# Causal attention of a fused four-stage kernel: its order of work across batches, its first scores and its start are rearranged

## What is computed

```python
q = frac_rope(einsum('btm,mhd->bhtd', x, wq)) * 128 ** -0.5    # H = 2 heads, D = 128
k = frac_rope(einsum('btm,mhd->bhtd', x, wk)) * 128 ** -0.5
v = einsum('btm,mhd->bhtd', x, wv)
s = einsum('bhid,bhjd->bhij', q, k) - 1e30 * (i < j)
p = softmax(s)
o = einsum('bhij,bhjd->bhid', p, v)
return einsum('bhid,hdm->bim', o, wo)

x = x + attn_a(layernorm(x))
x = x + ffn(layernorm(x))
x = x + attn_b(layernorm(x))
x = x + ffn(layernorm(x))
```

## Time and profile before

| what | value |
|---|---|
| median of 3 runs | 1931.45 us (1931.37 to 1933.29) |
| profiled execution | 1933.55 us, of which the span of its instructions 1931.8 us |
| granted TensorE clock, mean | 0.998 |
| TensorE busy | 1876.5 us, 97% of the span |
| VectorE busy | 1339.2 us, 69% |
| ScalarE busy | 878.5 us, 45% |
| GpSimd busy | 500.0 us, 26% |
| attention phase | to about 560 us of the span |

### The profile page before, as it was taken

The page is one execution under the profiler, slowest core; times in us unless marked ns, Lnnn a source line. Parts: engine busy times, 40 slices in busy tenths (PEclk is TensorE's granted clock), DMA queues, the critical chain, the costliest instruction groups (busy, mean ns, idle before and its releaser), DMA issues.

```text
span 1931.8 us, 36459 instructions
## 1 busy us (share of the span) xinstructions
PE 1876.5 (97%) x12321; PEld 1620.6 (84%) x12321; DVE 1339.2 (69%) x3141; ACT 878.5 (45%) x1716; POOL 500.0 (26%) x405
## 2 busy tenths in 40 slices
PE   6999999999999999999999999999999999899998
PEld 5778888887888888888888888888888887788887
DVE  5566666566668888766666766676766667788885
ACT  5666556555654444453333333333333332444443
POOL 4222102202222232232322222222222223422210
PEclk9999999999999999999999999999999999999999
DMA  7100000000013221120000000000000001222322
GB/s 240 41 1 0 0 0 0 0 0 0 6 22 84 33 31 29 29 70 10 10 11 10 11 11 11 11 11 11 11 11 11 12 12 15 38 62 62 64 57 54
DMA packets 230598, 53.19 MB, mean 28 GB/s; under 512 B 209664, under 2 KB 228736, under 8 KB 230144
## 3 DMA queue, kind: packets, MB, share of 16 engines
q1 hardware_dynamic: 229264, 49.53, 12.7%
q10 hardware_dynamic: 1264, 2.76, 0.4%
HBM read 18.69 MB, written 8.39 MB: 14 GB/s over the span
## 4 chain that ended last, share of the span: by engine, by line
PE 88%; DVE 4%; issue 2%; SPq 2%; ACT 1%; DMA 1%; POOL 1%; ACTq 0%; DVEq 0%; POOLq 0%
PE PS L324 18%; PE PS L1153 16%; PE PS L1162 9%; PE PS L333 7%; PE PS L815 6%; PE PS L844 6%; PE PS L1617 5%; PE PS L1659 4%; PE PS L1603 3%; PE PS L833 3%; PE PS L1636 3%; PE PS L1623 2%; PE PS L855 2%; SPq L272 2%; PE PS L1591 1%
## 5 line engine op out<-in xcount | busy, mean ns | idle before, releaser
L324 PE MATMUL PS<-ln_xh,lin_w 128*128 128x512 f32 x768 | 248.8, 392 | 0.0
L1090 ACT ACTIVATE ff_silu<-PS 128x512 f32<-128x512 f32 x192 | 114.5, 597 | 235.3 <-PE PS L1153 207.4
L1125 DVE SCALAR_TENSOR_TENSOR ff_h<-PS,ff_silu 128x512 f32<-128x512 f32 x192 | 131.3, 685 | 111.6 <-PE PS L1153 93.0
L1374 POOL TENSOR_TENSOR lin_yg_lo<-stage,lin_yg_hi 128x512 fp32r<-128x512 f32 x64 | 82.3, 1286 | 484.2 <-ACT lin_yg_hi L1392 484.2
L1392 ACT ACTIVATE lin_yg_hi<-stage 128x512 fp32r<-128x512 f32 x64 | 40.5, 633 | 347.4 <-DVE stage L1487 316.1
L1109 DVE TENSOR_TENSOR ff_h_lo<-ff_h,ff_h_hi 128x512 fp32r<-128x512 f32 x192 | 168.4, 877 | 0.4
L324 PEld LDWEIGHTS PS<-ln_xh,lin_w 128*128 128x128 f32 x768 | 144.2, 188 | 28.7
L844 PE MATMUL PS<-probT,v_a 128*128 128x128 f32 x1152 | 153.9, 279 | 3.7 <-DVE oT_lo L705 3.7
L844 PEld LDWEIGHTS PS<-probT,v_a 128*128 128x128 f32 x1152 | 139.0, 192 | 18.7 <-issue 11.1
L1449 DVE TENSOR_TENSOR lin_AD<-PS,lin_decay 128x512 f32<-128x512 f32 x128 | 82.2, 684 | 104.6 <-PE PS L1603 104.6
L324 PE MATMUL PS<-ln_xl,lin_w 128*128 128x512 f32 x384 | 150.1, 391 | 0.0
(11 more groups left out here) (172 smaller groups left out, 5187.8 us busy)
## 6 DMA issues: line engine op xcount, KB each, us to landing
ff_raw<-ln_xn SPq DMA_DIRECT2D x480, 32.0 KB, 2.0
ln_xl<-ln_xn SPq DMA_DIRECT2D x288, 32.0 KB, 1.9
X<-in_x SPq DMA_DIRECT2D x8, 1024.0 KB, 5.5
out_x<-X SPq DMA_DIRECT2D x16, 512.0 KB, 2.9
stage<-in_w_lin SPq DMA_DIRECT2D x1, 2048.0 KB, 8.2
stage<-in_w_gate SPq DMA_DIRECT2D x2, 768.0 KB, 7.4
stage<-in_w_up SPq DMA_DIRECT2D x2, 768.0 KB, 8.9
stage<-in_w_down SPq DMA_DIRECT2D x2, 768.0 KB, 10.3
```

The source lines that it names most:

```text
L324: last = nc.tensor.matmul(out, w, x, start=n == 0, stop=n == len(terms) - 1)
L1090: nc.scalar.activation(silu[:, f % NB_GU, :], PS[:, f % NB_GU, :], ACT.Silu, scale=W_SCALE).then_inc(silu_done.sem, 1)
L1125: nc.vector.scalar_tensor_tensor(h[:, f % 2, :], PS[:, NB_GU + f % NB_GU, :], W_SCALE, silu[:, f % NB_GU, :], ALU.mult, ALU.mult).then_inc ...
```

## The change

- Layernorm signals (statistics, aggregate, power) count once for each group of 4 tiles, and each of these steps is done for one group at a time. In the loop VectorE takes and aggregates group 0 at step 4 and group 1 at step 6.
- Start: x of batch 0 comes in two DMAs with a semaphore each; the identity has a semaphore of its own, and TensorE's first transposes wait for that alone; the first projection waits for two preparations, the other three are waited for before scores 0. VectorE's and ScalarE's preparations are reordered, the first half before `wo` and the mask.
- GpSimd adds the first half in two pieces, tokens 0 to 127 (`first_rotated`) and 128 to 511 (`rotated`).
- TensorE: scores 0 and 1 come before values 0 and 1; scores 0 wait for `first_rotated` and for the swap of projection 4, scores 2 for `rotated`. Values 2 come after scores 2. Transposes 0 and 1 wait for swaps 6 and 7.
- ScalarE: exponential 0 comes before values 0 and swap 7, and the copy of probabilities 0 before values 2.
- Weighted values 15 and output projection 14 of a batch come after the first projection of the next, output projection 15 after the second.
- First batch: squares after steps 8 to 15 and one behind the loop. Last batch: `low_sum` before the statistics, its transpose after projection 2.

```diff
@@ Layernorm
-    def dve_aggregate(self, dve, turn):
-        wait_alone(dve, self.stats_done.sem, self.stats_done.at(turn, 1), self.dve_passed)
-        for t in range(self.tiles):
+    def dve_aggregate(self, dve, turn, group=0):
+        wait_alone(dve, self.stats_done.sem, self.stats_done.at(turn, group + 1), self.dve_passed)
+        for t in range(group * UT, (group + 1) * UT):
...
@@ SP
-            load_x(0)
+            for half in range(NHALF):
+                at = slice(half * UT, (half + 1) * UT)
+                sp.dma_start(X[:, at, :], x_v[:, at, :]).then_inc(x_first[half], 16)
@@ GpSimd
-                        for h in range(HA):
-                            rows = slice(h * ROT, (h + 1) * ROT)
-                            done = nc.gpsimd.tensor_tensor(qk[rows, s, h, at], qk[rows, s, h, at],
-                                                           swapped[rows, 2 * half + s, :], ALU.add)
-                        done.then_inc(rotated.sem, 1)
+                        for some in (slice(0, P), slice(P, UN)) if half == 0 else (slice(0, UN),):
+                            for h in range(HA):
+                                rows = slice(h * ROT, (h + 1) * ROT)
+                                to = qk[rows, s, h, half * UN + some.start:half * UN + some.stop]
+                                done = nc.gpsimd.tensor_tensor(to, to, swapped[rows, 2 * half + s, some], ALU.add)
+                            done.then_inc((first_rotated if some.stop == P else rotated).sem, 1)
@@ ScalarE, start
+            act_decays(nc, act, env, 1)
+            sx[0].act(act, 0)
             act.wait_ge(const_loaded, 16 * N_CONST)
             nc.scalar.activation(wo_hi[:], wo_raw, ACT.Copy).then_inc(prep_hi, 1)
-            act_decays(nc, act, env, 1)
+            sx[1].act(act, 0)
@@ ScalarE, turn
                 for m in range(NPROJ - 1):
                     swap_halves(b, m)
+                exp_step(b, 0)
                 values(b, 0)
                 swap_halves(b, NPROJ - 1)
                 values(b, 1)
-                exp_step(b, 0)
                 for n in range(NS):
                     if n + 1 < NS:
                         exp_step(b, n + 1)
+                    evacuate_probs(b, n)
                     if n == 0:
                         values(b, 2)
-                    evacuate_probs(b, n)
...
-                    if first and n >= NS - NPART:
-                        part = n - (NS - NPART)
...
+                    if first and n > NS - NPART:
+                        square(n - (NS - NPART) - 1)
+                if first:
+                    square(NPART - 1)
                 evacuate_out(b, NS - 1)
@@ VectorE, turn
                 if last:
-                    following.ln.dve_stats(dve, 0)
                     dve.wait_ge(env["ff_squares"], NPART)
                     nc.vector.tensor_reduce(env["low_sum"][:], env["low_squares"][:], AX.X,
                                             ALU.add).then_inc(env["low_summed"], 1)
+                    following.ln.dve_stats(dve, 0)
@@ VectorE, start
+            for half in range(NHALF):
+                dve.wait_ge(x_first[half], 16)
+                ln.dve_stats(dve, 0, half)
             dve_decays(nc, dve, env, 1)
+            dve.wait_ge(prep_hi, 1)
             nc.vector.scalar_tensor_tensor(wqkv_lo[:, :, 0:nq], wqkv_raw[:, :, 0:nq], QK_SCALE,
                                            wqkv_hi[:, :, 0:nq].bitcast(F32), ALU.mult, ALU.subtract).then_inc(prep_done, 1)
+            ln.dve_normalise(dve, 0, 0)
+            dve.wait_ge(prep_hi, 2)
             nc.vector.tensor_tensor(wqkv_lo[:, :, nq:], wqkv_raw[:, :, nq:], wqkv_hi[:, :, nq:].bitcast(F32),
                                     ALU.subtract).then_inc(prep_done, 1)
+            ln.dve_normalise(dve, 0, 1)
+            sx[0].dve(dve, 0)
...
+            sx[1].dve(dve, 0)
             run_batches(dve, turn)
@@ TensorE, scores
-                if i % UT == 0 and h == 0:
+                if n == 0:
+                    pe.wait_ge(first_rotated.sem, first_rotated.at(b, 2))
+                elif n == HA or n == HA * UT:
                     pe.wait_ge(rotated.sem, rotated.at(b, 2 * (i // UT + 1)))
@@ TensorE, turn
-                pe.wait_ge(pt_done.sem, pt_done.at(b, 0))
...
                         if m == 0 and not first:
+                            weighted_values(b, -1)
+                            out_projection(b, -2)
+                        if m == 1 and not first:
                             out_projection(b, -1)
-                        if m == 0 and last:
+                        if m == 2 and last:
...
+                if first:
+                    pe.wait_ge(prep_done, 5)
+                pe.wait_ge(swap_done.sem, swap_done.at(b, NPROJ - 3))
+                scores(b, 0)
+                scores(b, 1)
                 values(b, 0)
                 pe.wait_ge(swap_done.sem, swap_done.at(b, NPROJ - 2))
                 values(b, 1)
-                scores(b, 0)
-                scores(b, 1)
-                values(b, 2)
-                pe.wait_ge(swap_done.sem, swap_done.at(b, NPROJ))
...
                 for n in range(NS):
+                    if n < 2:
+                        pe.wait_ge(swap_done.sem, swap_done.at(b, NPROJ - 1 + n))
                     transpose_probs(b, n)
                     if n + 2 == HA * UT:
                         pe.wait_ge(v_done.sem, v_done.at(b, TB))
                     if n + 2 < NS:
                         scores(b, n + 2)
+                    if n == 0:
+                        values(b, 2)
...
-                else:
-                    last_values()
-
-            pe.wait_ge(const_loaded, 16 * N_CONST)
+
+            pe.wait_ge(ident_loaded, 16)
             for s in sx:
                 s.pe(pe, 0, 0)
-            pe.wait_ge(prep_done, 5)
+            pe.wait_ge(prep_done, 2)
             run_batches(pe, turn)
```

More of the change, by code:

```diff
@@ L484, in attention_phase @@
         const_loaded, w_loaded, x_loaded = sem("a_const_loaded"), sem("a_w_loaded"), sem("x_loaded")
+        ident_loaded, x_first = sem("a_ident_loaded"), [sem(f"x_first{half}") for half in range(NHALF)]
         prep_hi, prep_done = sem("a_prep_hi"), sem("a_prep_done")
@@ L573, in turn @@
                 if not last:
-                    ln.pool_rstd(pool, b + 1)
+                    for half in range(NHALF):
+                        ln.pool_rstd(pool, b + 1, half)
                 else:
@@ L578, in turn @@
                     following.ln.pool_rstd(pool, 2)
-            ln.pool_rstd(pool, 0)
+            for half in range(NHALF):
+                ln.pool_rstd(pool, 0, half)
             run_batches(pool, turn)
@@ L795, in _ @@
             nc.vector.tensor_copy(mask_b[:], mask_f[:]).then_inc(prep_done, 1)
-            for s in sx:
-                s.dve(dve, 0)
+            sx[1].dve(dve, 0)
             run_batches(dve, turn)
```

91 lines of the change are left out of this document (42 added, 49 removed).

## The result

The changed kernel takes **1915.53 us** (median of 4 runs, 1914.17 to 1915.96), the kernel before, run beside it, 1931.41 (4 runs, 1929.85 to 1933.29). The ratio is 0.991, 95% interval 0.9899 to 0.9922. Forecast were 1918.8 and a range of 1912.5 to 1926. The profiled execution took 1915.64 with a span of 1913.9, against 1933.55 and 1931.8.

A forecast was written before the change was run, and what follows sets the result against it. TensorE, busy 97% of the span, was taken as the bound, its attention-phase waits as the room. Gains of 7.35 (batches), 1.9 (squares) and 3.4 (start) make 12.65, from the median 1931.45 to 1918.8 us; range 1912.5 to 1926.

The forecast's parts named there:

- The waits named: TensorE's waits in the attention phase: start, exponentials, attention output's low part, copied probabilities, low_sum; near 27 us in all.
- the signs named: Included no oT_lo wait, some 0.5 us before transpose 0, a new wait before values 3, period 66.2 us.
- Part 1: Deferred last values, run after the next batch's first projection: the 0.53 us wait goes seven times, 0.65 each with refill.
- Part 2: Early first scores with narrow rotation: transpose 1 sooner; with the deferral 1.0 us a batch, bounds 0 and 1.6.
- rival 2: Batch starts: both waits vanish because VectorE and ScalarE are a little quicker; 13.1 us there, 1913.0 us in all; chance 0.12.
- my own case: The whole forecast as summed: 1918.8 us, between 1914.5 and 1923; chance 0.71.
- Rival 1: Batch starts: GpSimd keeps its turn, times_sin(2) waits for all four key additions, nothing gained there; 1926.8 us; chance 0.14.
- Rival 3: GpSimd's narrow addition costs what a wide one does: at 1.3 us each the kernel takes 1956 us; chance 0.03.
- The last batch: Also loses the 0.9 us wait before low_sum, but VectorE's statistics delay the swaps; gain 1.0 us in all.
- Part 3: First batch's squares one step later: TensorE's wait for copied probabilities goes; gain 1.9 us, between 1.0 and 1.9.
- Part 4: Start: first projection at 15.7, 3.0 us earlier, plus 0.4 for the clock; gain 3.4 us, between 2.3 and 5.4.
- Part 5: The rest, such as norm signals by half at steps 4 and 6: cost 0.

The follow-up runs named there:

- n8: n1 plus one added wait: GpSimd adds the wide keys of the first half only after times_sin(2) is done; 1917.24 us.
- n1: Changed kernel with weighted values 15 and output projection 14 back at the end of their batch; 1922.39 us.
- n3: Changed kernel with only the keys of the first half split on GpSimd, the queries added in 512 columns again; 1917.79 us.
- n9: Changed kernel with one added wait alone: GpSimd adds the wide keys of the first half only after times_sin(2); 1915.85 us.
- n2: Changed kernel without the narrow addition: GpSimd adds queries and keys in 512 columns, scores 0 wait for the whole half; 1922.81 us.
- n4: Changed kernel with scores 0 and 1 and exponential 0 back at their old places, split, deferral and start kept; 1917.34 us.
- n7: Changed kernel plus three edits: wide keys wait for times_sin(2), both normalisations before the second low part of the weights, last batch's next-stage statistics at step 2; 1911.60 us.
- n5: Changed kernel with the first batch's squares back after steps 7 to 15; 1920.47 us.
- n10: The changed kernel again, letter for letter; 1915.39 us.
- n11: n7 again, the same program; 1914.82 us.

## Why the prediction was right or wrong

**Direction, range and bound: right.** The waits named were the room, and all of them went but the start's, which shrank. Of the signs named, two did not come: there is no wait before transpose 0, and the period is 65.62 and not 66.2. And one wait sits where the prediction called a wait a sign of being wrong, at scores 0, though in the last batch alone.

**Part 1: right, slightly small.** No wait for `oT_lo`; worth 0.72 a batch by n8, forecast 0.65. What the forecast did not have is that the deferral also shifts VectorE against GpSimd; without it, and without a guard, 0.66 more is lost (n1).

**Part 2 is where the sum fell short.** With Part 1 it gave 1.62 a batch for the 1.0 forecast, and of these 0.62 only 0.07 are Part 1's. The narrow price was right (0.458 for 0.48), and so was the time of the narrow keys. The step that failed is the one that laid `times_sin(1)` behind the whole query set, and with it "`times_sin(2)` enters at 100.95". I gave VectorE the gap at the second set of additions and not at the first, by the same rows. The distance from the first narrow query addition shows it: forecast 95.3 to `times_sin(2)` at 100.95, 5.65; measured 89.42 to 94.03, 4.61. `times_sin(1)` went into the gap between the two wide query additions and ended at 92.03, a full us sooner by the same count than behind the whole set, so the `times_cos` and swaps behind it were 0.6 to 0.85 us earlier, `times_sin(2)` was asked for a full us sooner, and TensorE found transpose 0 ready and values 3 all but ready. n3 is the kernel that I had laid out in this respect: `times_sin(1)` stands behind the whole query set again, and a batch gains 1.08 (67.24 less 66.16), which is nearly the forecast's 1.0.

That is the mechanism of **rival 2**, which I had given 0.12 and whose cause stood there in brackets. By the traces it is what happened in batches 1 to 6. Its 1913.0 was not reached since batch 0 lost the race (1.52; by n9 that is 0.56) and the last batch kept 0.9 us before scores 0. The two losses, 0.56 and 0.99, are 1.5 of the 2.5 us by which 1915.53 lies above rival 2. That it lies within the bounds of my own case (1914.5 to 1923) is luck to that extent: a larger gain in every batch than I had laid out, less two losses that rival 2 had not.

The Trainium skill, "SBUF — State Buffer", section "Who interferes with whom", says that the port pair which the two engines share is an exclusive lock and that the order of issue decides who is blocked. The traces agree: asked 0.01 us ahead `times_sin(2)` takes 0.68, asked 0.02 us behind it takes 1.52.

**Rival 1 fell** by `times_sin(1)` and `(2)` in the rows above. Even where VectorE asked too late (n1, batch 0 of the changed kernel) it waited for one addition and not for all four, and came in before the next. The row of `L1057`, which the prediction had set against it, says the same: in the trace of before, VectorE's `L1109` asked at 1655.24, inside GpSimd's addition of 1654.84, took 0.89, and GpSimd's next took 1.20. **Rival 3 fell** by 458 ns.

**What each half of Part 2 is worth** I had not separated. n2 and n4 do: without the cut a batch loses 1.1, without the early scores 0.42. The order of TensorE, which looks like the change, is the smaller part, the cut the larger. At least 0.54 of the cut's 1.1 is that VectorE is let in (n3); what of the rest is that and what is keys ready sooner was not separated. With the deferral's 0.72 the three losses make 2.2 where all together gained 1.62, so they are no shares of it.

**The last batch: 1.52 for 1.0.** The reason given was right, that VectorE's statistics delay the chain (n7: 1.35), only the size was off.

**Part 3: right in the sum (no wait left, as forecast), though not as a price.** The 1.9 was the wait's idle time; it cost 2.04 in the kernel before. With the other parts in place it is 4.35 (n5).

**Part 4: right.** First projection 15.65 for 15.7. I had priced the clock at 0.4; by the traces the eight projections took 12.50 us from first to last matmul against 13.02, 0.52. n10 makes them 11.47, which would be 1.55, so that the 0.4 was met is luck.

**Part 5: right.** No TensorE wait at steps 4 and 6.

The sum was 12.65, the medians differ by 15.88, the spans by 17.9. The gain at transpose 1 of batch 7 is 17.10, which is 4.45 over the sum: 0.07 by batch 0, 0.80 in batch 1, 3.06 in batches 2 to 6, 0.52 in batch 7. Batch 1 gained 3.70: 1.62 like the others and 2.04 for the squares' wait, with 0.04 left. That the medians differ by less than the traces is mostly that the profiled execution of before lay 2.1 above its median.

**Left open:** what the keys' cut does by the two ways named above; the three edits of n7, of which only the guard was run alone; why the part behind the attention phase differs by up to 4.4 us between traces; and the fall of the clock in n5, which one trace shows.

## What to carry to other kernels

Where two engines exclude each other, lay out both timelines for every one of their instructions, not only for the late one: the gap that opens at the second set opens at the first too, and a gain there moves everything behind it. Cutting one engine's long instructions can be worth as much by letting the other in as by what is ready earlier: here that was about half of the cut's 1.1 us a batch. Where the order of two requests hangs on hundredths of a us, one added wait that fixes it can be worth as much as a much larger edit (0.66 us a batch in n8), and any unrelated edit can flip it otherwise. The price of a stall isn't fixed either: in the kernel before it was 2.0 us, beside the other gains 4.35.

## What the runs showed of the hardware

- **VectorE and GpSimd.** In a gap between two GpSimd instructions that follow each other at once, VectorE's instruction with two SBUF inputs gets in. Asked 0.01 us or more ahead of GpSimd's next it takes 0.68 to 0.70 us; asked earlier, inside a GpSimd instruction, it ends 0.55 us behind that instruction (0.73 us long in batch 1, 0.83 in batch 3). GpSimd's next is stretched from 1.01 to between 1.37 and 1.53. Asked 0.02 or 0.04 us after the start of a 384-column addition, it takes 1.52. In batches 1 to 6 it falls the same way each time.
- **The clock after a stall.** After 2.73 us without work TensorE ran at 1.2 GHz for some 3 us (n5, granted clock 0.50); after 1.89 us (the kernel before, 1.00) it did not. That is one case of each.
- **The clock at the start.** With the first projection between 15.0 and 15.8 us, matmuls of 2.4 GHz began between 15.9 us (n3, n8) and 19.9 (n11), and for one and the same program at 17.3 and at 19.5 (n10, the changed kernel). The two executions are 1.0 us apart by this alone at the end of the projections, and the part behind the attention phase adds its own 1417.4 to 1421.8, so edits worth 1 or 2 us have to be judged by the same stretch of both traces, not by medians alone.
